# First rows of each stage normalised in the stage ahead, and the last heads' output products brought forward

## What is computed

```python
x = x + 0.5 * ffn(layernorm(x), w1, w2, w3)
x = x + attn(layernorm(x), Wq, Wk, Wv, Ww, cq, ck, cv, Wf1, Wf2, Wb, Wg1, Wg2, bg2, norm_w, Wo)
x = x + 0.5 * ffn(layernorm(x), w1, w2, w3)

def quantize(w):                       # ffn: weights to -1, 0, 1
    gamma = mean(abs(w)); return clip(round(w / (gamma + 1e-8)), -1, 1)
def ffn(x): return (sigmoid(x @ q(w1).T) * (x @ q(w2).T)) @ q(w3).T     # 512 -> 1408 -> 512

def attn(h):                           # 16 heads of 128, T = 512
    q, k, v, w = short_conv(h @ W.., c..)         # causal, 4 taps, silu
    g = log_sigmoid(h @ Wf1 @ Wf2); beta = sigmoid(h @ Wb); w = l2norm(w)
    # gated slot recurrence: Sk, Sv decay by exp(g), s = q Sk, a = softmax(s), o = a Sv
    o = rmsnorm(o) * norm_w * sigmoid(h @ Wg1 @ Wg2 + bg2)
    return o @ Wo
```

## Time and profile before

| | us |
|---|---|
| median of three timed runs | 2978.7 (2975.87 to 2978.82) |
| profiled execution | 2975.56 |
| its span, first to last instruction | 2973.5 |
| PE busy in the span | 2855.9 (96%) |
| DVE, ACT, POOL busy | 2166.2, 1614.9, 1339.5 |
| mean granted PE clock | 0.980 of full |

### The profile page before, as it was taken

One profiled execution on the slowest core, in us unless ns is written; L12 is line 12 of the kernel. 1 busy time (PEld: TensorE's weight loads), 2 busy tenths in 40 slices (PEclk: granted clock), 3 DMA queues, 4 the chain that ended last, 5 costly groups with the idle time before them and its releaser, 6 DMA issues. The chain is left out here.

```text
span 2973.5 us, 52631 instructions
## 1 busy us (share of the span) xinstructions
PE 2855.9 (96%) x18758; PEld 1887.1 (63%) x18758; DVE 2166.2 (73%) x5236; ACT 1614.9 (54%) x3682; POOL 1339.5 (45%) x1999
## 2 busy tenths in 40 slices
PE   5999699999999999999999999999999999987999
PEld 3888466666655666666656666666666666655887
DVE  6553488888885888888868888887788888863553
ACT  3111377666665666666666666666666666640110
POOL 0000456555554555555545555555455555550000
PEclk7999899999999999999999999999999999998999
DMA  6100311111111121111111211110112111105000
GB/s 236 69 15 15 112 41 37 37 47 34 47 33 57 48 65 34 47 33 50 30 57 47 66 33 50 37 48 25 43 55 60 37 49 32 55 16 187 15 15 29
DMA packets 89668, 151.64 MB, mean 51 GB/s; under 512 B 9152, under 2 KB 30784, under 8 KB 89024
## 3 DMA queue, kind: packets, MB, share of 16 engines
q1 hardware_dynamic: 89408, 148.29, 15.7%
HBM read 127.02 MB, written 21.23 MB: 50 GB/s over the span
## 5 line engine op out<-in xcount | busy, mean ns | idle before, releaser
L731 POOL TENSOR_TENSOR s<-s,tmp 128x256 f32<-128x256 f32 (+1 forms) x448 | 350.1, 782 | 321.3 <-DVE tmp L1026 291.7
L731 POOL TENSOR_TENSOR Y<-aT,D 128x256 f32<-128x256 f32 x384 | 277.7, 752 | 393.6 <-ACT aT L943 393.6
L731 POOL TENSOR_TENSOR X<-S,D 128x256 f32<-128x256 f32 x384 | 279.3, 727 | 171.2 <-ACT S L894 169.4
L1100 DVE COPY_PREDICATED A<-mask,ps 128x256 f32<-128x256 int32 x448 | 233.9, 522 | 104.4 <-issue 95.0
L217 ACT ACTIVATE sig<-up_ps 128x512 f32<-128x512 f32 x88 | 52.7, 599 | 472.4 <-PE up_ps L356 472.4
L356 PE MATMUL up_ps<-h_hi,wq 128*128 128x512 f32 x704 | 284.0, 403 | 10.5 <-DVE wq L276 9.5
L1345 PE MATMUL ps<-hT,slot_v 128*128 128x512 f32 x512 | 281.1, 631 | 0.0
L356 PE MATMUL up_ps<-h_lo,wq 128*128 128x512 f32 x704 | 280.2, 398 | 0.0
L1345 PE MATMUL ps<-hT,slot_q 128*128 128x512 f32 x512 | 274.4, 618 | 0.0
L1069 DVE SCALAR_TENSOR_TENSOR acc_k<-ps,tap,acc_k 128x511 f32<-128x511 f32 (+2 forms) x192 | 143.2, 746 | 177.4 <-ACT acc_k L877 175.0
L1345 PE MATMUL ps<-hT,slot_k 128*128 128x512 f32 x512 | 266.1, 605 | 1.3 <-ACT beta L866 1.3
(11 more groups left out here) (187 smaller groups left out, 6808.0 us busy)
## 6 DMA issues: line engine op xcount, KB each, us to landing
slot_k<-in_wk_dram SPq DMA_DIRECT2D x64, 256.0 KB, 2.6
slot_w<-in_ww_dram SPq DMA_DIRECT2D x64, 256.0 KB, 2.6
slot_q<-in_wq_dram SPq DMA_DIRECT2D x64, 256.0 KB, 2.6
slot_v<-in_wv_dram SPq DMA_DIRECT2D x64, 256.0 KB, 2.7
wo<-in_wo_dram SPq DMA_DIRECT2D x64, 256.0 KB, 3.4
wq_dram<-wq SPq DMA_DIRECT2D x3, 2816.0 KB, 23.4
wq<-wq_dram SPq DMA_DIRECT2D x9, 768.0 KB, 12.5
raw<-in_w_dram SPq DMA_DIRECT2D x8, 704.0 KB, 10.7
```

Of the source, the lines that this page charges most:

```text
L731: return nc.gpsimd.tensor_tensor(out, in0, in1, op)
L1100: nc.vector.copy_predicated(targets(A2, l), by_target(mask[l], l).bitcast(INT32), by_target(bank[f"a2_{l}"], l)).then_inc(dve_late, 1)
```

## The change

**Stage ends.** The identity matrix and `xn` become tiles of the whole kernel. The first feed-forward stage computes statistics and normalising of the first 512 rows of its result in its last block (m = 4 and 5), and attention does the same with the first 512 rows of x2 in its last turn (loaded in pass 49 of the SP loop). The stage after starts with the transposes. SP no longer waits for the stores at the end of the first two stages; where rows are read back from DRAM, SP waits first. POOL's identity and the waits of PE and ACT for the small weights go, except one ahead of f1.
**First feed-forward stage.** Pieces 1 to 3 of the third matrix are quantised behind hidden tiles 1, 2, 3, and `down_tile(0, 0)` goes behind `up_tile(0, 2)`.
**Second feed-forward stage.** Weight groups are tiles 0, 1, 2 to 3, 4 to 6, 7 to 10, each matrix waited for where it is used; rows of blocks 1 and 0 are loaded behind the third group.
**Last turn.** The output weights of the last four heads go into the slots k, w, q, v, which are free after the last projections. The products of heads 60 to 62 go into the last turn (`last_rows`), those of head 63 after it. The four products of group 14's last chunk are put together behind the transposes of s, and their addition ahead of merge 1.

```diff
-        groups = [(m, min(m + 3, MT)) for m in range(0, MT, 3)]
+        starts = [m for m in (0, 1, 2, 4, 7) if m < MT]
+        groups = list(zip(starts, starts[1:] + [MT]))
+        normed = [b + 1 for b in range(NB)] if not first else [b for b in range(NB + 1)]
+        if not first:
+            normed.pop()
...
-            load_rows(0)
             if first:
+                load_rows(0)
...
-                    if j == 1:
+                    if j == 2:
+                        sp.wait_ge(loaded, 16 * NB * C)
                         load_rows(1)
+                        load_rows(0)
...
-            sp.wait_ge(out_stored, 16 * NB)
             if first:
                 sp.wait_ge(wq_saved, 48)
+            else:
+                sp.wait_ge(stored, 16 * NB)
...
-            norm_stats(0)
-            norm_apply(0)
+            if first:
+                norm_stats(0)
+                norm_apply(0)
             split_norm(0, 0)
             split_norm(0, 1)
             if first:
-                for i in range(3):
+                for i in range(2):
                     threshold(i)
-                    quantise(i)
+                    for k in range(KT):
+                        quantise(i, k)
+                threshold(2)
+                quantise(2, 0)
             for b in range(NB):
                 for m in range(MT):
                     hidden(b, m)
+                    if first and b == 0 and 1 <= m < KT:
+                        quantise(2, m)
...
             def up_half(b, m, which):
+                if not first and b == 0 and m in starts:
+                    pe.wait_ge(wq_full[which][starts.index(m)], 16)
...
-                down_tile(0, 0)
             for b in range(NB):
                 for m in range(MT):
                     if not (first and b == 0 and m < 2):
                         up_tile(b, m)
+                        if first and b == 0 and m == 2:
+                            down_tile(0, 0)
...
-        last_bank = [psum[4], psum[0], psum[6], psum[1]]
+        last_bank = [psum[5], psum[7], psum[3], psum[1]]
...
-            sp.dma_start(xn[:, :, :], rows(x_in, 0)).then_inc(xn_full, 16)
...
             load_out_weights(0)
+            sp.wait_ge(loaded, 16 * NB)
             for c in range(C):
                 load_residual(0, c)
...
-                if u % NH == 1 and u // NH + 1 < NB:
+                if u % NH == 1:
                     sp.wait_ge(pe_edge, after(PE_EDGE, "lnT3", u // NH))
-                    sp.dma_start(xn[:, :, :], rows(x_in, u // NH + 1)).then_inc(xn_full, 16)
+                    if u // NH + 1 < NB:
+                        sp.dma_start(xn[:, :, :], rows(x_in, u // NH + 1)).then_inc(xn_full, 16)
+                    else:
+                        sp.wait_ge(res_stored, 16 * C * (NB - 2))
+                        sp.dma_start(xn[:, :, :], rows(x_out, 0)).then_inc(xn_full, 16)
...
-            load_out_weights(UNITS // C - 1)
+            for j, n in enumerate("kwqv"):
+                sp.wait_ge(pe_early, after(PE_EARLY, n, UNITS - 1))
+                sp.dma_start(wo_last[j][:, :], a["wo"][NH - C + j, :, :]).then_inc(wo_last_full, 16)
             for i in range(UNITS - C, UNITS):
                 store_residual(i)
-            sp.wait_ge(res_stored, 16 * NB * C)
...
-                stats = n // NH + 1 if n % NH == NH - 1 and n // NH + 1 < NB else None
+                stats = n // NH + 1 if n % NH == NH - 1 and n // NH + 1 < NB else NB if n == UNITS else None
...
+                if n == UNITS:
+                    residual(u - C, bank["out"])
...
-            pe.wait_ge(small_full, 16 * SMALL)
...
             def low_rank(b, name, wt):
+                if b == 0 and name == "f1":
+                    pe.wait_ge(small_full, 16 * SMALL)
...
+            def last_rows(c, *heads):
+                for j in heads:
+                    if j == C - 1:
+                        pe.wait_ge(dve_late, after(DVE_LATE, "og", UNITS - 1))
+                    mm = nc.tensor.matmul(last_bank[c][:, :], ck_(og[:, (UNITS - C + j) % (2 * C), :], c),
+                                          wo_last[j][:, :], start=(j == 0), stop=(j == C - 1))
+                    if j == C - 1:
+                        mm.then_inc(pe_out, 1)
...
                     scores(64, pe_late)
+                if n == UNITS:
+                    pe.wait_ge(wo_last_full, 16 * C)
+                    pe.wait_ge(dve_late, after(DVE_LATE, "og", UNITS - 2))
...
+                    last_rows(0, 0, 1, 2)
...
                     transpose("sT", lambda c: ck_(s, c), pe_late)
+                if n == UNITS:
+                    out_rows(u - C, bank["out"], 0, 1, 2, 3)
+                    pe.wait_ge(act_late, after(ACT_LATE, "sg", u))
+                    last_rows(1, 0, 1, 2)
...
                     chunk_outputs(pe_late)
+                if n == UNITS:
+                    pe.wait_ge(dve_out, UNITS - C)
+                    last_rows(2, 0, 1, 2)
+                    last_rows(3, 0)
...
                     transpose("onT", lambda c: on[:, c, :], pe_late)
+                if n == UNITS:
+                    last_rows(3, 1, 2)
...
             for c in range(C):
-                out_rows(UNITS - C + c, last_bank[c], 0, 1, 2, 3)
+                last_rows(c, C - 1)
```

More of the change, by code:

```diff
@@ L44, with ffn_phase @@
 Q_EPS = 1e-8
-def ffn_phase(nc, first, x_in, x_out, w_t, wq_dram):
+def ffn_phase(nc, first, x_in, x_out, w_t, wq_dram, ident, xn, loaded, stored):
     with ExitStack() as ctx:
@@ L67, in ffn_phase @@
         mhalf = sb("mhalf", [P, C])
-        ident = sb("ident", [P, P])
         ones = sb("ones", [P, P])
@@ L363, in up_tile @@
                 pair_free(("tile", b, m))
-                if not first and b == 0 and m % 3 == 0:
-                    for i in range(3):
-                        pe.wait_ge(wq_full[i][m // 3], 16)
                 up_half(b, m, 0)
@@ L374, in down_tile @@
                     pe.wait_ge(quantised, 2 * KT + ((m + 1) * HID - 1) // FF + 1)
+                if not first and b == 0 and m in starts:
+                    pe.wait_ge(wq_full[2][starts.index(m)], 16)
                 for c in range(C):
@@ L382, in down_tile @@
                 last.then_inc(down_done, 1)
-            pe.wait_ge(consts_ready, 5)
+            if first:
+                pe.wait_ge(consts_ready, 5)
             transpose_rows(0, 0)
@@ L523, in before, with attention_phase @@
     return u * len(steps) + len(steps)
-def attention_phase(nc, x_in, x_out, a):
+def attention_phase(nc, x_in, x_out, a, ident, xn, loaded, stored):
     with ExitStack() as ctx:
@@ L834, in turn @@
                     tt(r5[:, :], r4[:, :], rs[:, :]).then_inc(pool_late, 1)
-            deviation(0)
-            pool.wait_ge(dve_edge, after(DVE_EDGE, "xn3", 0))
             build_masks()
@@ L1275, in turn @@
                     end_state(2, dve_early)
-                if u >= C:
+                if u >= C and early:
                     residual(u - C, bank["out"])
-            row_stats(0)
-            norm_rows(0)
             dve.wait_ge(small_full, 16 * SMALL)
@@ L1585, in build @@
     ffn_w = (a["w1"], a["w2"], a["w3"])
-    ffn_phase(nc, True, a["x"], x1, ffn_w, wq_dram)
-    attention_phase(nc, x1, x2, a)
-    ffn_phase(nc, False, x2, out, ffn_w, wq_dram)
+    with ExitStack() as ctx:
+        ident = ctx.enter_context(nc.sbuf_tensor("ident", [P, P], FP32))
+        xn = ctx.enter_context(nc.sbuf_tensor("xn", [P, C, HID], FP32))
+        x_there, x1_stored, x2_stored, out_stored = (ctx.enter_context(nc.semaphore(n)) for n in (
+            "x_there", "x1_stored", "x2_stored", "out_stored"))
+        ffn_phase(nc, True, a["x"], x1, ffn_w, wq_dram, ident, xn, x_there, x1_stored)
+        attention_phase(nc, x1, x2, a, ident, xn, x1_stored, x2_stored)
+        ffn_phase(nc, False, x2, out, ffn_w, wq_dram, ident, xn, x2_stored, out_stored)
 def kernel(**inputs):
```

87 lines of the change are left out of this document (44 added, 43 removed).

## The result

| | before | after |
|---|---|---|
| timed runs, us | 2977.28 (2974.05 to 2978.82, 4 runs) | 2932.56 (2931.45 to 2932.70, 4 runs) |
| profiled execution, us | 2975.56 | 2932.70 |
| its span, us | 2973.5 | 2931.0 |

The ratio after / before is 0.9846, 95% interval 0.9835 to 0.9858: 1.5% faster. The forecast was 2931, with a range of 2921 to 2944.

A forecast was written before the change was run, and what follows sets the result against it. PE's waits at four places where a stage starts or ends were taken as the question. Gains 9.3 + 14.3 + 10.7 + 11.7 = 46.0 off 2975.56 gave 2929.6, plus half of 3.1: 2931, range 2921 to 2944.

The forecast's parts named there:

- the allowance of 1.5: Added to 2929.6: half of the 3.1 us by which the timed runs' median lay above the profiled execution.
- A: Start of first feed-forward stage: third quantisation spread over the first tiles lets PE restart sooner; gain 9.3 us (8 to 10).
- the cover over the rows of block 1: First feed-forward stage: hidden tile 5 ready about 1.5 us before PE wants it, despite later row loads.
- B: First feed-forward stage into attention: first block's rows normalised in the stage ahead; gain 14.3 us (11 to 15.5).
- the quick row: Attention's start: quickest row load, landing 2.6 us after issue; norm_w's landing was put near it, at 310.7.
- The middle: Attention's turns between its first projection and the last turn: left as they are, gain 0.
- rival 4: Attention's 63 turns: new tile addresses make DVE and PoolE disturb each other, 0.85 us a turn, 2985 us; chance 0.03.
- C: Last turn of attention: output products moved into the turn, tail of 17 us shrinks to 3.4; gain 10.7 (7 to 12).
- step (4): Last turn, chunk outputs to next stage: four head products, 3.4 us at full and 6.8 at lower clock, half of each.
- Rival 2: Last turn: head products between the steps only move the wait, gain 3, 2939 us; chance 0.20 together with Rival 1.
- D: Start of second feed-forward stage: rows already normalised, PE's steady products begin sooner; gain 11.7 us (10 to 12.5).
- Rival 1: Lower clock: last turn's seven products cost 6.0 us more, f1 with g1 3 more; 2940; chance 0.20 together with Rival 2.

The follow-up runs named there:

- undo_a: Changed kernel with only the third quantisation put back whole ahead of the hidden tiles, down tile 0 ahead of up tile 2; 2946.71 us, one run.
- store_waits: Changed kernel with the sync queue again waiting for its stores at the end of the first feed-forward stage and of attention; 2934.06 us, one run.
- small_early2: Changed kernel with attention's five small weights loaded in the first feed-forward stage, into memory the quantisation no longer needs; 2931.70 us, ratio to before 0.9838.
- both_orders: Changed kernel, last turn: statistics and normalising moved later on VectorE, three head products spread singly over TensorE's waits; 2923.83 us, ratio to before 0.9814.
- undo_products: Changed kernel with only the last turn's output products back in their old places; last turn 49.24 us instead of 37.35, span 2942.7, one run.
- pe_order: Changed kernel with three head products of the last turn moved from ahead of au's transposes to behind level 16's outputs; 2932.03 us, one run.
- groups_of_three: Changed kernel with the last stage's quantised weights loaded in groups of three tiles again, rows of block 1 behind two groups; 2934.29 us.
- same_again: The changed kernel run once more, unaltered; 2933.18 us, ratio to before 0.9853.
- kept_busy: Changed kernel with six unread products of 512 columns given to PE among the transposes of attention's first turn; 2935.42 us, ratio to before 0.9856.

## Why the prediction was right, and where its terms were not

The time, 2931 against 2932.56, and the range were right. The closeness is in part luck. The four terms sum to 46.0 where 42.5 were measured between the two profiled executions' spans; the allowance of 1.5 from the profiled execution to the median, put on the forecast for another reason, covered a part of that.

**A** was right in size (9.4 for 9.3) and in its steps: tile 3 at 54.4 for 54.6, pieces behind the hidden tiles, and the cover over the rows of block 1 held (DVE waited, PE did not). undo_a shows the one cause.

**B** was 3.0 short (11.3 for 14.3), in two terms. First the landing of the small weights. norm_w was issued 4.1 after the store, as I had it within 0.1, but landed 4.1 later, and not 2.8. I had taken the quick row because "1 MB of store that has landed at 308.0" would be out of the way; the store took 5.3, was still under way at norm_w's issue, and store_waits shows the quick landing (2.8) only with a store that has landed. That is 1.3. Second the clock at f1: 0.5 was allowed, 2.2 was lost (13.14 for 10.93), because the clock fell during the transposes and came back only near 307. I had read the earlier trace rows, one stretch with the clock up, as a property of the place; the executions since range from 10.90 to 14.46. small_early2 takes that wait away and gives 18.29, a gain of 14.4. That it meets the 14.3 of the forecast is chance: its terms are 5.90 and 12.39, where I had 7.0 and 11.4.

**The middle** didn't move, so rival 4, from the new addresses, is refuted: the same 63 turns took 2313.51 and 2313.57.

**C** was right in its mechanism and 0.9 too large. PoolE's wait was 2.23 for 2.2, au's transposes came 13.2 after the addition for 13.3, the chunk outputs 22.6 for 22.5. Two sizes were off. Normalising took 3.49 and not 2.7, beside PoolE, but the merges behind it caught up 1.6 and not 1.0. And in step (4) I had the four head products on the path, partly at the lower clock. They were not on it: PE was through with them and idle for 0.45 when VectorE's on released the transposes. What was long were the chunk outputs ahead of them, at the lower clock, 3.15 us against 2.03 before and 1.6 in both_orders. So on's transposes came 30.0 after the addition where I had 29.2. Rival 2, that head products only move the wait, is refuted by undo_products (11.9), though it named a true cost: pe_order won back 2.5 of it, 1.5 of these by the clock.

**D** was right (12.3 for 11.7): no wait for weights in the first execution, and groups_of_three shows that the smaller first groups are 1.6 of it. That the store's wait at the end of attention costs 1.7 was within the term.

**Rival 1**, the lower clock, happened in part: at f1 by 2.2 of its 3, not in the seven products of C, which ran at the full clock (3.60 for eight records).

## What to carry to other kernels

Where a step is put into a turn to be hidden, put it where its engine waits for others, not where its input happens to be ready: the same statistics, normalising and three products took 8.4 us less in one order than in another. Small loads at a stage's start are paid by their landing beside whatever is still under way, so their issue moved up by 2.6 here and won 1.3; loading them a stage ahead won 3.1 at its place. And judge a change at its place, cut at the same events in both traces: executions of one kernel differed by 3.5 us in a stretch that the change never touched. A stretch of low clock that comes back at the same place in every execution, as behind the betas at the three later edges, deserves a run of its own; none was made here.

## What the runs showed of the hardware that I had not expected

- The granted clock falls to 1.2 GHz while PE idles for no more than 0.31 us (at 314.5 in same_again, 313.6 in kept_busy), in or just behind 32 records of 16 columns: at the first edge in six of the thirteen profiled executions, at each of the three later edges in all thirteen. A stretch lasts 3.4 to 6.9 us. Why the first edge differs from one execution to the next is open, and no run moves or drops these 32 records to show that they bring the fall.
- In the changed kernel PE's last product ended at 291.7, the transposes began at 295.57, and the clock stayed at 1.00 until 296.8, so that it looks as if the transposes brought it down. Other executions show that the gap is enough: in same_again, undo_a, pe_order and store_waits the clock fell while PE was idle, ahead of the first transpose. In same_again:

```profile
294.00:294.20 0.20, 0.00 (x0) 0.67 0.76 287
...
294.43 4.01 PE L1316 MATMUL ps<-ident,xn 128*128 128x128 f32 x16 [3.85 <-DVEq L1040]
```

- Four normalisings of 128x512 took 3.49 beside PoolE and 1.88 without it; PoolE's six took 4.99 and 4.28.
- A 0.5 KB load landed after 4.1 behind a 1 MB store under way, after 2.8 behind one that had landed.
